# An attention, convolution and Hartley-transform kernel: its first image stacked on chip head by head, a projection on 32x32 tiles, box sums on GpSimd, fillers among the first maxima

## The chip, the cores and the metric

One core of a Trainium2 chip runs the kernel. The metric is the device time of one execution in microseconds (us), lower is better; three runs of the kernel before gave a median of 336.1 us (335.73 to 336.81).

## The reference

`x` is (4, 32, 32, 32), float32. Four blocks follow one another, each `x = x + block(norm(x))`, the norm one over each image and channel:

- block 0: a 3x3 convolution with first- and second-order (Volterra) products of its taps
- block 1: a 3x3 convolution
- block 2: one step of a convolutional LSTM whose gates come from attention
- block 3: a 2-D Hartley transform, a mix of 32x32 modes, the transform back

Block 2, which the change is about, with its hidden state at zero:

```
xin = W_in x + b_in
q = conv3x3(xin, 'SAME')        # 4 heads of 8 channels, 1024 queries
k, v = conv3x3(xin, 'VALID')    # 900 keys
a = softmax(q k) v
```

The pair (h, xin) has zero queries, so its attention is the mean of its values over all keys, a constant for each image: it needs only the nine sums of x over the 30x30 windows. Gates, cell, hidden state and `W_out` follow.

## The kernel before

There is one instruction stream for each engine; semaphores join them. An attention "half" is one image (of 4) and one half of the queries (512 of 1024), eight in all, in the order `divmod(s, 4)`: first query half of images 0 to 3, then the second.

*Front of block 2.* After the norm (`padded`, L778) TensorE projects x to `xin` (L1073 to L1079): 24 matmuls of 128 rows, one for each image, query half and vertical shift, float32, which the profile shows as two passes each. ScalarE (L644) and VectorE (L783) evict them in turn into `xst`; GpSimd blanks two edge rows (L578, L582). `conv` (L1081) then makes K, Q and V (L1098, L1101, L1108), each in two halves. The window sums of the constant are six VectorE reductions (L791, L795); three small chains of matmuls on TensorE turn them into a bias of the gates: `win_done` (L1100), 36 one-column matmuls (L1106), 12 more (L1113).

*Splitting.* So that bf16 matmuls keep float32 accuracy, Q and K are split into three bf16 parts each: ScalarE copies (L648 to L662), VectorE subtracts (L800 to L829). K is kept as its 900 keys and as the difference of its two halves. The nine products of parts are nine groups of 8 rows, 72 in all, laid out ("stacked") in `qst` and `kst`. SyncE writes the parts to DRAM (`k_scratch` L492, `q_scratch` L495) and loads the stacks from there (`stack_k` L503, `stack_q` L511), the first image in two pieces, then all others; the second query half is written (L528) and stacked last. TensorE transposes the values (L1119, L1124), and VectorE copies them out (L839 to L847), before the first maximum.

*Maxima and scores.* A softmax needs the largest score of each query. A "max block" (L1140) is 128 queries against 450 keys, four matmuls beside each other on 32-column tiles. As a pair: ScalarE takes the Relu of the difference block (L683), VectorE adds it to the first half's block and reduces (L877). The other blocks VectorE reduces alone (L882). When a half has its 16 maxima they are split, turned on TensorE (L1150), copied (`mt_sb`, L891), and one GpSimd DMA (L596) puts them below that half's queries as rows 72 to 74; its semaphore is `m_in`. Only then can the half's scores start: `score_tile` (L1169, L1174) makes 128 keys x 512 queries, ScalarE takes the exponent (L675), and `values` (L1187, L1193) accumulates in float32, 128 rows high.

*Order.* `attention_plan()` writes one list that each engine walks. It takes the 32 blocks and turn of the first half and 18 blocks of the second (`FIRST_AHEAD`), then gives each step of scores 4.15 blocks. A turn is moved behind the next four blocks (`MOVED`). `block_bank` hands out PSUM banks: six until the prologue's end, then three.

```python
    take(2 * ROWS_OF_MAX + 1 + FIRST_AHEAD)
...
                plan.append(("score", s * EXP_UNITS + t * HEADS + h))
                k = int(due * (h + 1) / units + 1e-6)
                take(k - taken)
```

`keep_clock` (L999) runs matmuls on zeros whose result nobody reads. In the last half the gates of the first query halves are worked off as items between the steps (L1244, L921 to L932).

## Time and profile before

| | us |
|---|---|
| median of three runs | 336.1 |
| the profiled execution, its own time | 335.8 |
| its span | 334.0 |
| TensorE / VectorE / ScalarE / GpSimd busy | 298.5 / 216.7 / 175.8 / 40.7 |
| mean granted clock of TensorE, 1.0 being 2.4 GHz | 0.952 |

How to read it: PE is TensorE, PEld its weight loads, DVE VectorE, ACT ScalarE, POOL GpSimd, SPq the DMA issues of SyncE. A matmul's end is modelled, so a busy TensorE is not one at its peak. In a line of the timeline stand start, duration, engine, line, operation, output and input, the count, and in brackets the idle time before it and what ended it. In a line of the windows stand the stretch and its length, then busy us and instructions of PE, PEld, DVE, ACT and POOL, the granted clock (PEclk), the mean busy share of the 16 DMA engines and GB/s. In a group's line stand the count, busy us and mean ns; a line's own view gives min/median/max ns and first and last start.

### The profile page before, as it was taken

How to read it: one execution, taken by the hardware profiler on the slowest of the kernel's cores; microseconds unless marked ns; L12 is line 12 of the kernel's file. 1: busy time of each engine (PE TensorE's matmuls, PEld its weight loads, DVE VectorE, ACT ScalarE, POOL GpSimd, SP SyncE). 2: the span in 40 equal slices, each digit the busy share in tenths (PEclk: the TensorE clock that was granted, in tenths of full speed). 3: DMA queues.
4: the chain of work that ended last, by engine and by line, in shares of the span. 5: the costliest groups of instructions: out<-in, count | busy, mean ns of one | idle time of the engine just before them, and what ended most of it. 6: DMA issues, size and time to landing. Idle time of an engine off the chain costs nothing. (4 is left out here: it accounts for less than half of the span.)

```text
span 334.0 us, 9963 instructions
## 1 busy us (share of the span) xinstructions
PE 298.5 (89%) x4276; PEld 130.9 (39%) x4283; DVE 216.7 (65%) x484; ACT 175.8 (53%) x338; POOL 40.7 (12%) x50
## 2 busy tenths in 40 slices
PE   5899979899798599999999999999997998895893
PEld 2577523234332244334334344344342223344731
DVE  3991263486497138687878878888773223779935
ACT  1201110324375479788988979889797983100000
POOL 8400000000000000100101001010200108007000
PEclk9999999999965579999999999999999999997999
DMA  7000000007796469300000000000000000000001
GB/s 265 36 4 4 7 5 1 2 0 202 169 148 109 127 182 327 140 3 4 2 5 2 3 4 2 4 4 2 4 2 4 3 0 2 0 2 2 4 0 63
DMA packets 3471, 15.40 MB, mean 46 GB/s; under 512 B 731, under 2 KB 1547, under 8 KB 2883
## 3 DMA queue, kind: packets, MB, share of 16 engines
q1 hardware_dynamic: 3171, 14.67, 16.2%
q8 instruction: 33, 0.54, 0.7%
q0 software_dynamic: 256, 0.11, 0.2%
q14 instruction: 11, 0.09, 0.1%
HBM read 12.21 MB, written 2.37 MB: 44 GB/s over the span
## 5 line engine op out<-in xcount | busy, mean ns | idle before, releaser
L675 ACT ACTIVATE arena_b<-ps 128x512 f32<-128x512 f32 x232 | 125.3, 609 | 26.2 <-PE ps L1169 24.6
L1140 PE MATMUL ps<-arena_a 72*32 72x450 bf16 x1024 | 93.7, 390 | 3.0 <-DVE vrest L847 0.8
L1169 PE MATMUL ps<-arena_a 75*32 75x512 bf16 x896 | 88.4, 390 | 6.2 <-DMA arena_a<-mt_sb 5.5
L882 DVE TENSOR_REDUCE mx<-ps 128x1 f32<-128x450 f32 x120 | 68.5, 616 | 2.8 <-PE ps L1140 2.8
L877 DVE CUSTOM_DVE_ANT_0 sums<-ps,relus 128x450 bf16<-128x450 f32 x68 | 41.8, 625 | 36.8 <-PE ps L1140 30.5
L1187 PE MATMUL ps<-arena_b,vt 128*32 128x512 f32 x448 | 59.0, 601 | 1.0 <-ACT arena_b L675 1.0
L1140 PEld LDWEIGHTS ps<-arena_a 72*32 72x32 bf16 x1024 | 28.7, 102 | 53.7 <-DVE mx L882 16.0
L1169 PEld LDWEIGHTS ps<-arena_a 75*32 75x32 bf16 x896 | 24.5, 97 | 49.8 <-ACT arena_b L675 23.1
L683 ACT ACTIVATE relus<-ps 128x450 f32<-128x450 f32 x68 | 37.5, 554 | 8.3 <-PE ps L1140 7.4
L1029 PE MATMUL ps<-arena_a,cst 32*32 32x512 f32 x864 | 28.6, 596 | 1.1 <-ACT arena_a L626 1.1
L999 PE MATMUL ps<-zeros 128*128 128x512 bf16 x82 | 21.3, 397 | 6.5 <-DMA xa<-x 3.5
L1029 PEld LDWEIGHTS ps<-arena_a,cst 32*32 32x32 f32 x864 | 20.7, 103 | 8.7 <-issue 2.6
L596 POOL DMA_DIRECT2D arena_a<-mt_sb x8 | 5.2, 651 | 104.8 <-DVE mt_sb L891 104.8
L1187 PEld LDWEIGHTS ps<-arena_b,vt 128*32 128x32 f32 x448 | 13.7, 111 | 7.4 <-ACT arena_b L675 2.3
L743 DVE SCALAR_TENSOR_TENSOR arena_a<-xp 128x612 f32<-128x612 f32 (+1 forms) x24 | 16.2, 753 | 0.0
L632 ACT ACTIVATE arena_b<-ps 128x512 f32<-128x512 f32 x4 | 2.2, 596 | 26.6 <-PE ps L1029 26.6
L1088 PE MATMUL ps<-arena_b,cst 128*32 128x450 f32 (+1 forms) x144 | 15.8, 564 | 0.0
L999 PEld LDWEIGHTS ps<-zeros 128*128 128x128 bf16 x89 | 8.0, 100 | 18.6 <-issue 7.7
L1285 PE MATMUL ps<-arena_b,arena_a 128*64 128x64 f32 x256 | 9.8, 245 | 4.7 <-DVE arena_a L458 4.6
L603 POOL TENSOR_TENSOR on<-ot,rden 128x512 f32<-128x512 f32 x7 | 7.3, 1041 | 54.4 <-DVE rden L901 54.4
L458 DVE TENSOR_TENSOR arena_a<-arena_a 32x256 f32<-32x256 f32 x24 | 12.9, 563 | 0.5
L899 DVE STREAM_TRANSPOSE ot<-ps 128x512 f32<-128x512 f32 x8 | 5.7, 713 | 10.1 <-PE ps L1193 10.1
(140 smaller groups left out, 237.3 us busy)
## 6 DMA issues: line engine op xcount, KB each, us to landing
arena_b<-wmodes SPq DMA_DIRECT2D x1, 4096.0 KB, 21.0
arena_a<-k_scratch SPq DMA_DIRECT2D x3, 516.8 KB
arena_a<-q_scratch SPq DMA_DIRECT2D x3, 384.0 KB
cst<-consts SPq DMA_DIRECT2D x1, 1045.0 KB, 8.6
k_scratch<-arena_b SPq DMA_DIRECT2D x3, 344.5 KB, 3.7
cst<-consts SPq DMA_DIRECT2D x1, 864.5 KB, 6.5
arena_a<-k_scratch SPq DMA_DIRECT2D x6, 129.2 KB
arena_a<-k_scratch SPq DMA_DIRECT2D x3, 258.4 KB
```

The lines of the kernel that those rows point to most:

```text
L458: return engine.tensor_tensor(dst, v, u, ALU.subtract if part else ALU.add)
L675: nc.scalar.activation(probs[:, n % PRING, :], ps[:, SCORE_RING[n % len(SCORE_RING)], :], ACT.Exp).then_inc(expd, 1)
L683: nc.scalar.activation(relus[:, d % 3, :], ps[:, block_bank(i), 0:KHALF], ACT.Relu).then_inc(max_relu, 1)
L743: nc.vector.scalar_tensor_tensor(maps[:, m, n0:n1], xp[:, n0:n1], VOLTERRA_SCALE, xp[:, at + n0:at + n1], ALU.mult, ALU.mult).then_inc(map ...
L877: nc.vector.tensor_tensor_reduce(out=sums[:, d % 2, :], in0=bank, in1=relus[:, d % 3, :], scale=1.0, scalar=-3.0e38, op0=ALU.add, op1=ALU.max,
L882: nc.vector.tensor_reduce(mx[:, a, e:e + 1], bank, AX.X, ALU.max).then_inc(max_read, 1)
L999: mm(ps[:, bank, :], zeros[:, 0:P], zeros[:], start=True, stop=True)
L1029: last = mm(ps[32 * j:32 * j + 32, 2 * b + e, :].rearrange("p (y x) -> p y x", x=W), l0w[r, COL_TILES * i + j, :], window(maps[r, m, :], p ...
L1088: last = mm(ps[32 * b:32 * b + 32, bank + e, 0:ny * cols].rearrange("p (y x) -> p y x", x=cols), weights[:, px, :], window(xst[:, b, :], f ...
L1140: last = mm(ps[32 * j:32 * j + 32, block_bank(i), 0:KHALF], qst[0:PAIR_ROWS, e, g, q0:q0 + 32], kst[0:PAIR_ROWS, g, at:at + KHALF], start= ...
L1169: last = mm(ps[32 * j:32 * j + 32, bank, :], kst[0:S_ROWS, g, k0:k0 + 32], qst[0:S_ROWS, e, g, :], start=True, stop=True)
L1187: last = mm(ps[32 * h:32 * h + 32, bank, :], vt[:, t, half % B * HEADS + h, :], probs[:, (n0 + h) % PRING, :], start=(t == 0), stop=False, ...
```

## The change

Constants are laid out anew: in `kst` and `k_parts` the difference stands first, then the 900 keys. The parts are:

- *Projection*: 24 matmuls on 32x32 tiles, each image's rows by its own 32x32 weights, eight banks.
- *Order of the halves*: `HALVES`, image 0's first and second query half, then images 1 to 3, first halves before second.
- *Convolutions*: Q, K, K, Q, V, V by halves, each split as soon as it is out.
- *Stacks of image 0*: straight from `q_parts` and `k_parts` on chip, one DMA for each head and part: Q heads 0 and 1 and K from SyncE, Q heads 2 and 3 from GpSimd. The last keys of K (the second 450, of use to scores only) come in twelve further DMAs. GpSimd issues the writes to DRAM. Images 1 to 3 are loaded from DRAM once the first `m_in` has landed.
- *Box sums*: 18 chained additions on GpSimd, halving the row each time, then column corrections.
- *Window chain* (mean, value, gate), bias of `W_out` (`bout`): items of the plan in the last half; gates and what follows move two steps later.
- *Values' transposes*: items among the first maxima, copied out by ScalarE, the rest by VectorE.
- *Fillers*: matmuls on zeros, 128 rows on four 32-column tiles: 256 columns behind each pair of the first half's last eight, and behind each pair of the second half's first nine; four of 512 before the first score.
- *Turn*: the first half's is no longer moved.
- *Banks*: six for the first 32 blocks, four for the 19 that follow, then three.
- `ident_b`, `mx` and the ones of `vt`, `vrest` are set on GpSimd earlier.

```diff
 KPAD = DT * P + 32
-KDIFF = KPAD
-KW = KPAD + KHALF
-K_RANGES = (slice(0, KPAD), slice(KDIFF, KW))
+KDIFF = 0
+KEY0 = KHALF
+KW = KEY0 + KPAD
+K_SECOND = slice(KEY0 + KHALF, KW)
...
 O_RING = (6, 7)
+EARLY_RING = (3, 4, 5, 7, 0, 2)
+AHEAD_RING = (3, 4, 5, 7)
+XIN_BANKS = (0, 1, 2, 6, 3, 4, 5, 7)
+K_BANKS, Q_BANKS, V_BANKS = (0, 1), (2, 6), (0, 1)
+VT_TILES = 3
...
 FIRST_AHEAD = 18
-WIDE_AHEAD = 12
 BLOCKS_PER_STEP = 4.15
 MOVED = 4
+AMONG_FIRST = {2: (("vt", 0),), 3: (("vt_copy", 0),), 6: (("vt", 1),), 7: (("vt_copy", 1),)}
+PAIRED = 2
+FILLS_BEFORE = 4
 MODE_STAGES = [(k2, lh) for k2 in range(2) for lh in range(2)]
...
             for kind in (("diff", "first") if pair else ("first", "second")):
                 stream.append(("max", i, s, a, kind))
                 i += 1
+            if s == 0:
+                stream += AMONG_FIRST.get(a, ())
+            if s == 0 and a > max(AMONG_FIRST):
+                stream.append(("fill", 256))
         stream.append(("split", s))
         stream.append(("turn", i, s))
...
-    take(2 * ROWS_OF_MAX + 1 + FIRST_AHEAD)
+    take(2 * ROWS_OF_MAX + 1)
+    for _ in range(FIRST_AHEAD // 2):
+        take(2)
+        plan.append(("fill", 256))
+    plan += [("fill", 512)] * FILLS_BEFORE
     due, prev, later, step = 0.0, None, [], 0
...
-                    later += [(step + 1, ("gates", 0)), (step + 2, ("cell", 0)), (step + 3, ("hidden", 0)),
-                              (step + 4, ("out", 0))]
+                    later += [(step, ("window", "mean")), (step, ("bout",)), (step + 1, ("window", "value")),
+                              (step + 2, ("window", "gate")), (step + 3, ("gates", 0)), (step + 4, ("cell", 0)),
+                              (step + 5, ("hidden", 0)), (step + 6, ("out", 0))]
...
-            ring = SCORE_RING + MAX_RING if i < prologue else MAX_RING
+            last = 2 * ROWS_OF_MAX
+            ring = EARLY_RING if i < last else AHEAD_RING if i < last + 1 + FIRST_AHEAD else MAX_RING
...
+            def stack_q_head(g):
+                for s in range(PARTS):
+                    sp.dma_start(qst[part_rows(s), 0, g, :],
+                                 q_parts[HC * g:HC * (g + 1), s, 0:HALF].unsqueeze(1).to_broadcast([HC, PARTS, HALF])
+                                 ).then_inc(q_head[g], 16)
...
+            def stack_k_head(g, cols, signal):
+                for s in range(PARTS):
+                    sp.dma_start(kst[part_rows(s), g, cols], k_parts[HC * g:HC * (g + 1), :, cols]).then_inc(signal, 16)
...
+            for s in range(PARTS):
+                sp.wait_ge(q_part[s], 1)
+            for g in range(2):
+                stack_q_head(g)
             for s in range(PARTS):
                 sp.wait_ge(k_part[s], 2)
-                if s == 0:
-                    sp.wait_ge(k_zeroed, 2)
-                sp.dma_start(k_dram[:, s].rearrange("c g n -> g c n"), k_parts[:, s, :]).then_inc(kd_written, 16)
+            for g in range(HEADS):
+                stack_k_head(g, slice(0, K_SECOND.start), k_head[g])
+            sp.wait_ge(qd_written[1], PARTS * 16)
+            stack_q(1, 0, HEADS, q_second)
+            sp.wait_ge(k_padded, 1)
+            sp.wait_ge(k_zeroed, 1)
             for s in range(PARTS):
-                sp.wait_ge(q_part[s], 1)
-                sp.dma_start(q_dram[s, 0].rearrange("c g n -> g c n"), q_parts[:, s, 0:HALF]
-                             ).then_inc(qd_written[0], 16)
...
+                sp.wait_ge(k_part[s], 3)
+            for g in range(HEADS):
+                stack_k_head(g, K_SECOND, k_second)
+            sp.wait_ge(m_in, 16)
             sp.wait_ge(kd_written, PARTS * 16)
-            stack_k(0, 0, HEADS // 2)
             sp.wait_ge(qd_written[0], PARTS * 16)
-            stack_q(0, 0, 0, HEADS)
-            stack_k(1, HEADS // 2, HEADS)
...
-            stack_q(3, 1, 0, G)
+            for b in range(1, B):
+                stack_k(b)
+                stack_q(0, HEADS * b, HEADS * (b + 1), q_in[b - 1])
+            stack_q(1, HEADS, G, q_in_second)
             sp.wait_ge(ones_in, 16)
-            sp.wait_ge(m_in, 16)
+            for g in range(HEADS):
+                sp.wait_ge(q_head[g], PARTS * 16)
+                sp.wait_ge(k_head[g], PARTS * 16)
+            sp.wait_ge(k_second, HEADS * PARTS * 16)
             sp.dma_start(wm, wmodes).then_inc(wm_loaded, 16)
...
+            pool.wait_ge(vt_zeroed, 2)
+            nc.gpsimd.memset(vt[:, :, :, HC:HC + 1], 1.0).then_inc(vt_zeroed, 1)
+            for h in range(HEADS):
+                pool.wait_ge(vt_zeroed, 3 + h)
+                nc.gpsimd.memset(vrest[32 * h:32 * h + KREST, :, 32 * h + HC:32 * h + HC + 1], 1.0
+                                 ).then_inc(vt_zeroed, 1)
...
+            nc.gpsimd.memset(k_parts[:, :, KEY0 + KEYS:KW], 0.0).then_inc(k_zeroed, 1)
+            nc.gpsimd.memset(mx[:], -3.0e38).then_inc(mx_ready, 1)
+            pool.wait_ge(consts_loaded, 16)
+            nc.gpsimd.tensor_copy(ident_b[:], c_("ident")).then_inc(mx_ready, 1)
...
-            pool.wait_ge(vt_ready, 2 + HEADS)
             pool.wait_ge(xin_ready, 2)
-            nc.gpsimd.memset(vt[:, :, :, HC:HC + 1], 1.0).then_inc(vt_zeroed, 1)
...
+            def win_link(out, a, b, op):
+                win_steps[0] += 1
+                nc.gpsimd.tensor_tensor(out, a, b, op).then_inc(win_step, 1)
+                pool.wait_ge(win_step, win_steps[0])
...
+            win_link(cols[:, :, 0:n], image[:, :, 0:n], image[:, :, n:2 * n], ALU.add)
+            while n > 1:
+                n //= 2
+                win_link(cols[:, :, 0:n], cols[:, :, 0:n], cols[:, :, n:2 * n], ALU.add)
+            for v, (x0, x1) in enumerate(((30, 31), (0, 31), (0, 1))):
+                win_link(wsum[:, v, :].unsqueeze(2), image[:, :, x0:x0 + 1], image[:, :, x1:x1 + 1], ALU.add)
+            win_link(wsum[:], cols[:, :, 0:1].rearrange("p y x -> p x y").to_broadcast([P, 3, H]), wsum[:], ALU.subtract)
...
+            for s in range(PARTS):
+                pool.wait_ge(q_part[s], 1)
+            for g in range(2, HEADS):
+                for s in range(PARTS):
+                    pool.dma_start(qst[s * PARTS * HC:(s + 1) * PARTS * HC, 0, g, :],
+                                   q_parts[HC * g:HC * (g + 1), s, 0:HALF].unsqueeze(1).to_broadcast([HC, PARTS, HALF])
+                                   ).then_inc(q_head[g], 16)
+            for s in range(PARTS):
+                pool.dma_start(q_dram[s, 0].rearrange("c g n -> g c n"), q_parts[:, s, 0:HALF]).then_inc(qd_written[0], 16)
+            for s in range(PARTS):
+                pool.wait_ge(q_part[s], 2)
+                pool.dma_start(q_dram[s, 1].rearrange("c g n -> g c n"), q_parts[:, s, HALF:HW]).then_inc(qd_written[1], 16)
+            for s in range(PARTS):
+                pool.wait_ge(k_part[s], 3)
+                pool.dma_start(k_dram[:, s].rearrange("c g n -> g c n"), k_parts[:, s, :]).then_inc(kd_written, 16)
...
+            first, diff, second = (slice(KEY0, KEY0 + KHALF), slice(KDIFF, KDIFF + KHALF), slice(KEY0 + KHALF, KEY0 + KEYS))
+            act.wait_ge(q_done, 1)
+            q_copy(0, 0, ps[:, Q_BANKS[0], :])
+            act.wait_ge(q_left, 1)
+            q_copy(1, 0, q_res[:, 0:HALF])
+            act.wait_ge(k_done, 1)
+            nc.scalar.activation(k_first, ps[:, K_BANKS[0], 0:KHALF], ACT.Copy).then_inc(k_copied, 1)
+            act.wait_ge(k_copied, 1)
+            k_copy(0, first, k_first)
+            act.wait_ge(k_left, 1)
+            k_copy(1, first, k_res[:, first])
+            act.wait_ge(k_left, 2)
+            k_copy(0, diff, k_res[:, diff])
             act.wait_ge(k_done, 2)
...
-                act.wait_ge(dve_step, Q_RESID[e])
-                nc.scalar.activation(q_parts[:, 1, half], q_res[:, half], ACT.Copy).then_inc(q_part[1], 1)
-            act.wait_ge(v_done, 2)
...
-            nc.scalar.activation(vs.rearrange("p (a n) -> p a n", a=2), ps[:, 6:8, 0:KHALF],
-                                 ACT.Copy).then_inc(vs_ready, 1)
+            k_copy(0, second, ps[:, K_BANKS[1], 0:KHALF])
+            act.wait_ge(k_left, 3)
+            k_copy(1, diff, k_res[:, diff])
+            act.wait_ge(q_done, 2)
+            q_copy(0, 1, ps[:, Q_BANKS[1], :])
+            act.wait_ge(k_left, 4)
+            k_copy(1, second, k_res[:, second])
+            act.wait_ge(q_left, 2)
+            q_copy(1, 1, q_res[:, HALF:HW])
+            v_copy(0)
+            v_copy(1)
             for item in plan:
                 if item[0] == "score":
...
+            dve.wait_ge(q_part[0], 1)
+            q_rest_of(0)
+            dve.wait_ge(q_part[1], 1)
+            q_last(0)
+            dve.wait_ge(k_part[0], 1)
+            k_rest_of(first, k_first, 0)
+            dve.wait_ge(k_done, 2)
+            nc.vector.tensor_tensor(k_res[:, diff], ps[:, K_BANKS[1], 0:KHALF], k_first, ALU.subtract).then_inc(k_left, 1)
+            dve.wait_ge(k_part[1], 1)
+            k_last(first)
+            dve.wait_ge(k_part[0], 2)
+            dve.wait_ge(k_left, 2)
+            k_rest_of(diff, k_res[:, diff], 0)
+            dve.wait_ge(k_part[1], 2)
+            dve.wait_ge(k_left, 3)
+            k_last(diff)
+            dve.wait_ge(k_part[0], 3)
+            k_rest_of(second, ps[:, K_BANKS[1], 0:KHALF], 0)
+            dve.wait_ge(q_part[0], 2)
+            q_rest_of(1)
+            dve.wait_ge(k_part[1], 3)
+            dve.wait_ge(k_left, 4)
+            k_last(second)
+            dve.wait_ge(q_part[1], 2)
+            dve.wait_ge(q_left, 2)
+            q_last(1)
             def split_max(s):
...
+            def keep_clock_tiled(bank, n):
+                for j in range(COL_TILES):
+                    mm(ps[32 * j:32 * j + 32, bank, 0:n], zeros[:, 0:32], zeros[:, 0:n], start=True, stop=True)
...
-                e, b = divmod(n, B)
+            for e in range(2):
                 for r in range(3):
-                    last = mm(ps[32 * r:32 * r + 32, (2 + n) % 8, :].rearrange("p (y x) -> p y x", x=W),
-                              c_("win")[:, 32 * b:32 * b + 32],
-                              window(xp, r, 1, 16 * e, 16, W), start=True, stop=True)
-                last.then_inc(xin_done, 1)
-            def conv(bank, weights, rows, cols, first, signal):
+                    for b in range(B):
+                        rows = slice(32 * b, 32 * b + 32)
+                        last = mm(ps[32 * r:32 * r + 32, XIN_BANKS[e * B + b], :].rearrange("p (y x) -> p y x", x=W),
+                                  c_("win")[rows, rows], window(xp[rows], r, 1, 16 * e, 16, W), start=True, stop=True)
+                        if r == 2:
+                            last.then_inc(xin_done, 1)
...
+            pe.wait_ge(xin_ready, 1)
+            conv(Q_BANKS[0], qkv[:, 0], H, W, 0, q_done, 0)
+            conv(K_BANKS[0], qkv[:, 1], KH, KH, 1, k_done, 0)
+            pe.wait_ge(xin_ready, 2)
+            conv(K_BANKS[1], qkv[:, 1], KH, KH, 1, k_done, 1)
+            conv(Q_BANKS[1], qkv[:, 0], H, W, 0, q_done, 1)
+            pe.wait_ge(k_copied, 1)
+            conv(V_BANKS[0], qkv[:, 2], KH, KH, 1, v_done, 0)
+            pe.wait_ge(k_left, 4)
+            conv(V_BANKS[1], qkv[:, 2], KH, KH, 1, v_done, 1)
...
+            def of_window(what):
+                bank = WIN_BANKS[("mean", "value", "gate").index(what)]
+                if what == "mean":
+                    pe.wait_ge(win_step, WIN_STEPS)
+                    for i in range(len(MAX_RING)):
+                        pe.wait_ge(*blocks_read[turn_of[2 * B - 1] - i])
+                    mm(ps[:, bank, 16:25], c_("win"), win9[:, 0, :], start=True, stop=True).then_inc(win_done, 1)
...
+            def turn_values(part):
+                if part == 0:
+                    pe.wait_ge(vs_ready, 1)
+                    pe.wait_ge(q_left, 2)
+                    for t in range(VT_TILES):
+                        last = nc.tensor.transpose(ps[:, 6, t * P:(t + 1) * P], vs[:, t * P:(t + 1) * P], c_("ident"))
+                else:
...
                     max_block(*item[1:])
                 elif item[0] == "turn":
                     turn_maxima(*item[1:])
+                elif item[0] == "vt":
+                    turn_values(item[1])
+                elif item[0] == "fill":
+                    if not fills:
+                        pe.wait_ge(vt_ready, 2)
+                    fills.append(item)
+                    keep_clock_tiled(V_BANKS[1], item[1])
...
+                            if bank in EARLY_RING:
+                                pe.wait_ge(*blocks_read[block_before(2 * ROWS_OF_MAX, bank)])
+                        pe.wait_ge(vt_ready, 2)
+                        pe.wait_ge(vrest_ready, HEADS)
                         pe.wait_ge(vt_zeroed, 3 + HEADS)
+                        pe.wait_ge(k_second, HEADS * PARTS * 16)
```

## Rows read from the trace of the kernel before

**Rows 1.** Windows by stage, columns as told in the profile section.
```profile
59.98:88.97 28.99, 26.66 (x307) 10.76 (x309) 16.73 (x33) 9.29 (x14) 1.00 (x3) 1.00 0.35 94
88.97:112.59 23.62, 17.45 (x202) 5.91 (x202) 15.97 (x56) 13.45 (x25) 1.39 (x6) 0.60 0.73 129
112.59:134.20 21.61, 21.45 (x274) 9.15 (x278) 11.07 (x32) 18.14 (x37) 0.60 (x1) 0.80 0.76 238
134.20:255.80 121.60, 118.18 (x1814) 46.96 (x1804) 97.06 (x234) 105.65 (x208) 10.07 (x12) 1.00 0.03 10
255.80:276.30 20.50, 19.24 (x214) 5.63 (x206) 4.46 (x7) 17.86 (x35) 1.05 (x2) 1.00 0.01 2
```

**Rows 2.** Timeline, all engines, from the first split to the first values.
```profile
100.17 0.19 DVE L854 TENSOR_REDUCE negm<-mx 128x16 f32<-128x32 f32 x1
...
102.79 0.79 POOL L596 DMA_DIRECT2D arena_a<-mt_sb  x1 [12.99 <-DVE mt_sb L891]
...
112.62 0.62 PE L1169 MATMUL ps<-arena_a 75*32 75x512 bf16 x4 [5.17 <-DMA arena_a<-mt_sb]
...
118.19 1.95 PE L1187 MATMUL ps<-arena_b,vt 128*32 128x512 f32 x8
```

**Rows 3.** The DMAs that carry the turned maxima, line 596.
```profile
L596 POOL DMA_DIRECT2D arena_a<-mt_sb x8: 603/637/785, 102.8 to 254.8; - x8
...
DMA to landing us min/median/max: 2.0/2.8/9.6
```

**Rows 4.** Timeline from the projection to the first maxima.
```profile
59.98 6.66 PE L1076 MATMUL ps<-xp,cst 128*32 128x512 f32 x45 [1.31 <-DVE xp L728]
...
62.06 0.75 DVE L783 TENSOR_SCALAR arena_b<-ps,cst 96x512 f32<-96x512 f32 x1 [2.13 <-PE ps L1076]
...
72.83 5.36 PE L1088 MATMUL ps<-arena_b,cst 128*32 128x512 f32 x48
...
80.18 4.84 PE L1088 MATMUL ps<-arena_b,cst 128*32 128x450 f32 x48
...
88.97 1.51 PE L1140 MATMUL ps<-arena_a 72*32 72x450 bf16 x28 [0.77 <-DVE vrest L847]
```

**Rows 5.** The page's groups: the first convolution.
```profile
L1029 PE MATMUL ps<-arena_a,cst 32*32 32x512 f32 x864 | 28.6, 596 | 1.1 <-ACT arena_a L626 1.1
```

**Rows 6.** Timeline of the splitting of the query projection.
```profile
78.47 0.63 ACT L662 ACTIVATE arena_b<-arena_b 128x512 bf16<-128x512 f32 x1 [1.45 <-DVE arena_b L822]
...
79.20 0.69 DVE L829 TENSOR_TENSOR arena_b<-arena_b 128x512 bf16<-128x512 f32 x1 [0.77 <-ACT arena_b L662]
```

**Rows 7.** SyncE's issues of the key stacks, line 503.
```profile
L503 SPq DMA_DIRECT2D arena_a<-k_scratch x12: 342/365/462, 81.6 to 90.5; - x12
```

**Rows 8.** Timeline of the window matmuls.
```profile
78.12 2.13 PE L1106 MATMUL ps<-win,cst 32*32 32x1 f32 x72
```

**Rows 9.** Timeline, VectorE's reads of maxima, at either clock.
```profile
91.22 0.62 DVE L877 CUSTOM_DVE_ANT_0 sums<-ps,relus 128x450 bf16<-128x450 f32 x1
91.76 0.62 DVE L877 CUSTOM_DVE_ANT_0 sums<-ps,relus 128x450 bf16<-128x450 f32 x1
...
96.50 0.63 DVE L877 CUSTOM_DVE_ANT_0 sums<-ps,relus 128x450 bf16<-128x450 f32 x1
...
97.25 0.63 DVE L877 CUSTOM_DVE_ANT_0 sums<-ps,relus 128x450 bf16<-128x450 f32 x1
```

**Rows 10.** Windows, TensorE alone: busy, clock, DMA share, GB/s.
```profile
94.00:98.00 4.00, 4.00 (x48) 0.50 1.06 168
...
121.00:124.00 3.00, 3.00 (x52) 0.98 1.09 284
```

**Rows 11.** GpSimd's normalisation by form, and VectorE's mode parts beside GpSimd's.
```profile
L603 POOL TENSOR_TENSOR on<-ot,rden 128x512 f32<-128x512 f32 x7 | 7.3, 1041 | 54.4 <-DVE rden L901 54.4
...
L458 DVE TENSOR_TENSOR arena_a<-arena_a x24: 409/417/940, 300.7 to 313.7; 32x256 f32<-32x256 f32 x24
```

**Rows 12.** The page's DMA issues: key stack of one image.
```profile
arena_a<-k_scratch SPq DMA_DIRECT2D x3, 258.4 KB
```

348 lines of the change are left out of this document (171 added, 177 removed).

## The prediction

> **What bounds the kernel now.** I read the windows by stage first [rows 1]. From 134.2 to 255.8 us TensorE is busy 118.2 of 121.6 us at full clock: six halves of the attention loop, 20.3 us each, run at what the engine can do. The weak stage is 88.97 to 112.59, the first maxima alone: TensorE 17.5 of 23.6 us, mean clock 0.60, DMA share 0.73. Then I read the timeline where it ends [rows 2]. GpSimd issues the DMA with the first turned maxima at 102.79, and the first score waits for it until 112.62. Its landing is the slowest of eight, 9.6 us against a median of 2.8 [rows 3]; it shares the DMA engines with the stacks of all images. Before this stage the first maximum starts at 88.97 [rows 4], behind the projection (from 59.98), three convolutions, the splitting, the trip through DRAM and the transposes of the values. The loop has no slack, so the end moves with the start of the first score, T1 = 112.6.
>
> **Projection to first maximum.** 24 matmuls of 128 rows take 6.66 us [rows 4]. On 32x32 tiles the nearest row is the first convolution, 864 passes in 28.6 us, 33 ns each [rows 5]. Twelve matmuls are 24 passes, 0.8 us, and about 0.3 us until the first arrives: one half is out at 61.1, both by 62. Now the evictions bound it: VectorE's four at 0.75 [rows 4] end at 61.1 + 3.1 = 64.2 with their handovers, ScalarE's four beside them. Two on each engine and GpSimd's small memset, some 0.3 (three instructions take 1.00 us there [rows 1]), release the first convolution at 63.1 instead of 66.1.
> TensorE then runs Q, K, K, Q, V, V. A half of 512 columns costs 2.6 (5.36 for two [rows 4]), one of 450 costs 2.4 (4.84 for two [rows 4]). Ends: 65.7, 68.1, 70.5, 73.1, 75.5, 77.9.
> The splits are links of 0.63 on ScalarE and 0.69 on VectorE [rows 6], each behind the other. First Q half: four links from 65.7, ready at 68.4. K's first half and the difference: the last needs K's second half (70.5), then five links, the engines crossing, so 73.8. The V convolutions wait for the copy of K's first half and for its last remainder (74.4); both are there before TensorE is. SyncE then issues twelve K copies. A K stack's issue takes 0.37 [rows 7], GpSimd's up to 0.79 [rows 3]; I take 0.5, nearer the first. Head 0's three are out at 75.3 and land by the median of 2.8 at 78.1; bounds 77.9 (TensorE) and 85 (at 9.6). With the engines nearly empty I take the median. Maxima start at **78.1**, 10.9 us earlier. Window matmuls (2.13 us [rows 8]) and value transposes no longer stand in front.
>
> **First half's maxima.** Sixteen pairs at 0.55, VectorE's start to start at full clock [rows 9], 8.7 us; the first read comes 1 us after the first matmul; two value copies on ScalarE (0.63 each as in [rows 6]) add 1.2, with VectorE's rest copies beside them. End 89.0. A pair costs TensorE 0.75 at half clock, where it is never idle (4.0 of 4.0 us [rows 10]), so 0.38 at full; it idles 0.17 of 0.55, and a filler of 256 columns (0.11) fits: nothing. Split, turn and copy took from 100.17 to 102.79 with two reads between [rows 2]; without them 1.6: 90.6. As the turn is no longer moved behind later blocks, TensorE stands still for some 1.3 us of that.
>
> **Queues.** GpSimd's 18 box-sum steps read 1300 elements a partition: at 2.0 ns (512 in 1.04 us [rows 11]) and 0.2 a step 6.2 us, so 64.9 to 71.1. Lower bound 2.7 (by elements alone), upper 18.7 (1.04 for every step). Most steps have under 100 elements, so I take 6.2; the upper end would make head 2 land at 88 where it is wanted at 83, 5 us lost. Behind the sums stand six Q head copies, six Q writes and three K writes, 15 issues at 0.64 [rows 3], out by 81. The second Q half's write has landed by 84, SyncE stacks it by 89, wanted at 90.6: a cover of 1.6 us; if it goes, each us late is a us of T1. K's last columns, twelve more copies, land by 95. Behind SyncE's new wait for the first m_in stand all stacks of images 1 to 3. M_in: 90.6 + 0.64 + 2.2 = 93.5 on a quiet queue (2.0 to 9.6 [rows 3]).
>
> **Second half's maxima.** Nine pairs before the first score. With four banks a pair needs its predecessors' back, which I estimate at 0.62 a pair: 5.6 us, and four fillers of 512 columns 0.85. **T1 = 97.0**, 15.6 us earlier; bounds 93.5 (m_in) and 103 (m_in at 9.6).
>
> **After T1.** (a) Until 121 the clock was at half [rows 10]. Still the first half took only 21.6 us against 20.3 later [rows 1], because ScalarE is nearly as full: at full clock it gives back 1.3 (bounds 0 and ScalarE's idle 3.5). (b) The window chain moves into the last half, where ScalarE is busy 17.9 of 20.5 us and fed by TensorE [rows 1]: 2.13 + 0.6 us of one-column matmuls, of which the score banks hide about 1: 1.7 lost (bounds 0 and 2.8). VectorE has 16 idle us there: bias add and small copies cost nothing. (c) Image 1's stacks, 3 x (258.4 [rows 12] + 96) KB, at 129 GB/s [rows 1] take 8.2 us from 95: there by 106, wanted at 108. The second m_in is issued near 110 among the others; at 9.6 us it lands at 120, wanted at 118: 1.0 lost (bounds 0 and 2).
>
> **Sum.** 335.8 (the profiled execution; its span is 334.0) - 15.6 - 1.3 + 1.7 + 1.0 = 321.6. The runs' median is 336.1, so plus 0.3: **321.9 us**.
>
> [...] From 94 to 98 TensorE is never idle at half clock and stays there; before it fell it had run maxima for 0.38 of each 0.55 us, behind pauses. Four-pass matmuls come in at 118.19 [rows 2], and by 121 the clock is up [rows 10]. Whether the fillers hold it among maxima no row shows, hence two rivals, and by these rows a clock once lost stays lost to the first values. [...]
>
> **Rivals.**
> 1. *The clock falls in the turn's gap,* 89 to 91. For: it fell at 94 after the pauses between 85.0 and 88.97 [rows 4] and thin maxima. Against: fillers on both sides. At half clock a pair with its filler is 0.75 + 0.21 = 0.96: nine pairs cost 3.1 more, the four fillers 0.85, and (a) is lost, 5.2 together: **327.1**.
> 2. *It falls among the first eight pairs,* which have no fillers; two rounds of four-pass transposes speak against. Ten more pairs at 0.96 add 4.0: **331.1**.
> 3. *Slower: GpSimd's queue.* M_in stands behind 15 issues of d us: T1 = 71.1 + 15d + 2.9. With (a) lost, break-even is at T1 = 109.9, d = 2.4. Against: eight issues took 0.60 to 0.79 beside VectorE's maxima [rows 3]. For: those moved 12 KB each, and a VectorE operation with two inputs in SBUF went from 0.41 to 0.94 us beside GpSimd [rows 11], so the two do block each other. At d = 3 T1 is 118.9 and the time **345**. The Trainium skill (SBUF — State Buffer, A bandwidth-pool intuition that's wrong) has such a DMA go from about 620 to 3100 ns beside a VectorE copy; by that figure the time would be about 346, an estimate. No row here shows it.
> 4. *Better:* the pairs pack tighter and m_in alone sets T1 = 93.5, 3.5 less: **318.4**.
> 5. *The stacks come late:* head or second-half stacks share the DMA engines with the K writes and each is 2 us later: **326**, inside the range.
>
> **How the numbers follow.** Forecast 0.42, rival 1 0.22, rival 2 0.12, rival 3 0.04, rival 4 0.08, rival 5 0.12. Rivals 1 and 5 lie above, so the range is lopsided: 316.5 (rival 4 with its 2 us of spread) to 331.5 leaves out rival 3, half of rival 2 and the tails. A measurement of this kernel tells about 0.3%, 1 us, from no change. Faster 0.94, same 0.02, slower 0.04: only GpSimd's queue near or beyond d = 2.4 is not faster.
>
> **What would show it.** First maximum near 78; VectorE's reads 0.55 apart to 89; the second m_in landing late. Granted clock 1.0 from 78 to 130, or 0.5 from about 91 (rival 1) or 83 (rival 2). GpSimd's issues near 0.64 and m_in issued right behind the copy, or rival 3. First score near 97, and from there to the last score about 165 us (163.2 now, 112.6 to 275.8). The forecast is wrong if that length changes by over 3 us, or if the heads land after 80.

## The result, and the profile after

The kernel with the change takes **336.28 us** (median of 20 runs, 333.14 to 341.14), the kernel before, measured beside it, 337.37 (20 runs, 335.73 to 341.93). The ratio is **0.9934**, 95% interval 0.9906 to 0.9963: 0.7% faster, where 4.2% was forecast. The time lies above the range. Ratios, here and below, are taken over undisturbed runs and medians over all, so the two need not agree exactly.

| us | before | forecast | after (profiled) |
|---|---|---|---|
| profiled execution / span | 335.8 / 334.0 | | 337.8 / 336.0 |
| projection starts | 59.98 | 59.98 | 61.60 |
| first maximum | 88.97 | 78.1 | 80.20 |
| GpSimd issues the first maxima DMA | 102.79 | 90.6 | 100.57 |
| first score, T1 | 112.6 | 97.0 | 109.8 |
| first to last score, the loop | 163.2 | about 165 | 168.5 |

T1 is 12.8 later than forecast and the loop 3.5 longer: 321.6 + 12.8 + 3.5 = 337.9, the profiled execution. By the table the 12.8 are 2.1 at the first maximum, 7.9 from there to the DMA's issue (forecast 12.5, now 20.4) and 2.8 from that to T1 (6.4, now 9.2).

Windows by stage, the kernel after; columns as in [rows 1]:

```profile
59.93:80.20 20.27, 17.16 (x194) 5.26 (x193) 10.90 (x18) 9.76 (x17) 13.21 (x29) 1.00 0.15 24
80.20:90.00 9.80, 5.07 (x83) 2.66 (x87) 5.35 (x20) 4.80 (x10) 3.93 (x8) 0.94 0.78 217
90.00:100.50 10.50, 8.53 (x106) 4.53 (x105) 6.18 (x22) 4.40 (x9) 0.00 (x0) 0.50 0.26 62
100.50:109.79 9.29, 9.29 (x120) 4.65 (x116) 5.71 (x18) 4.90 (x9) 0.62 (x1) 0.52 0.57 118
...
131.00:152.00 21.00, 17.08 (x230) 6.42 (x234) 12.85 (x32) 13.43 (x27) 1.48 (x2) 0.84 0.46 153
```

The first line is the part that came out about as forecast. In the second, where the sixteen pairs should be going at 0.55 each, TensorE is busy for only half of the time while the DMA engines are busy for 0.78 of it. From 89, inside that hole in TensorE's work, the clock is at its lower level, 1.2 GHz, until the first score. The last line holds a second hole. TensorE's timeline shows both:

```profile
61.60 2.21 PE L1212 MATMUL ps<-xp,cst 32*32 32x512 f32 x48 [1.34 <-DVE xp L850]
64.76 14.62 PE L1222 MATMUL ps<-arena_b,cst 128*32 128x512 f32 x144 [0.95 <-POOL arena_b L629]
80.20 0.57 PE L1296 MATMUL ps<-arena_a 72*32 72x450 bf16 x8 [0.82 <-DMA arena_a<-arena_b]
...
89.87 0.94 PE L1296 MATMUL ps<-arena_a 72*32 72x450 bf16 x8 [4.24 <-issue]
...
99.74 0.28 PE L1306 MATMUL ps<-ident_b,mparts 128*32 128x128 bf16 x2 [1.97 <-DVE mparts L967]
...
109.79 0.40 PE L1323 MATMUL ps<-arena_a 75*32 75x512 bf16 x4
...
134.84 0.62 PE L1323 MATMUL ps<-arena_a 75*32 75x512 bf16 x4 [3.88 <-DMA arena_a<-mt_sb]
```

The projection is down from 6.66 us [rows 4] to 2.21. Before the first pair of head 2, at 89.87, TensorE stands still for 4.24 us with no releaser named; the turn's gap is 1.97; and at 134.84 a score waits 3.88 for the second half's maxima DMA (of which the group of line 687 says the same: it landed 11.1 us after its issue, where before the slowest was the first, 9.6 [rows 3]).

```profile
L687 POOL DMA_DIRECT2D arena_a<-mt_sb x8: 616/624/646, 100.6 to 254.9; - x8
...
DMA to landing us min/median/max: 2.0/2.1/11.1
```

GpSimd's queue, where the slower rival was looked for, in its timeline:

```profile
66.07 1.32 POOL L641 TENSOR_TENSOR on<-xp 128x512 f32<-128x512 f32 x1
67.47 1.97 POOL L641 TENSOR_TENSOR on<-on 128x256 f32<-128x256 f32 x4
...
75.80 3.62 POOL L670 DMA_DIRECT2D arena_a<-arena_b  x6 [0.31 <-POOL win L641]
79.38 1.62 POOL L674 DMA_DIRECT2D q_scratch<-arena_b  x3
80.99 1.57 POOL L677 DMA_DIRECT2D q_scratch<-arena_b  x3
82.56 1.57 POOL L680 DMA_DIRECT2D k_scratch<-arena_b  x3
```

Fifteen issues in 8.3 us, 0.56 each: the queue is fast. But see what it issues when: from 79.38 to 84.13 nine writes to DRAM. Now SyncE in the same stretch (line 531: key columns of one head and one part, on chip):

```profile
70.42 4.33 SPq L524 DMA_DIRECT2D arena_a<-arena_b  x6
75.50 13.34 SPq L531 DMA_DIRECT2D arena_a<-arena_b  x12
88.88 2.64 SPq L544 DMA_DIRECT2D arena_a<-q_scratch  x3
91.71 8.55 SPq L531 DMA_DIRECT2D arena_a<-arena_b  x12
```

Twelve copies, three for each head in turn, take 13.34 us: the first seven 0.7 each, the other five, from 80.50 on, 1.0 to 2.7. By this head 2's third copy was issued by 83.2, and its first pair still stood until 89.87, with nothing in the wait list that says why. That its keys landed late is an inference here. Whether SyncE's issue by itself is slow or the writes slow the copies is what the first experiment asks.

### The profile page after: what moved, and what is told of

Same layout as the page of the kernel before. It is cut to its first block and busy times, and to the rows that moved or that the text cites. A ratio compares the mean times of both kernels' runs of the same rounds, so it can differ in the third digit from the quotient of the medians.

```text
span 336.0 us, 10195 instructions
## 1 busy us (share of the span) xinstructions
PE 296.6 (88%) x4358; PEld 134.4 (40%) x4364; DVE 212.4 (63%) x476; ACT 176.7 (53%) x343; POOL 57.7 (17%) x84
## 3 DMA queue, kind: packets, MB, share of 16 engines
HBM read 11.12 MB, written 2.37 MB: 40 GB/s over the span
## 5 line engine op out<-in xcount | busy, mean ns | idle before, releaser
L1296 PE MATMUL ps<-arena_a 72*32 72x450 bf16 x1024 | 95.3, 389 | 6.9 <-issue 4.7
L1323 PE MATMUL ps<-arena_a 75*32 75x512 bf16 x896 | 86.8, 386 | 4.7 <-DMA arena_a<-mt_sb 3.9
L1343 PE MATMUL ps<-arena_b,vt 128*32 128x512 f32 x448 | 58.1, 593 | 0.5 <-ACT arena_b L786 0.5
L1296 PEld LDWEIGHTS ps<-arena_a 72*32 72x32 bf16 x1024 | 29.4, 102 | 54.3 <-issue 20.8
L1323 PEld LDWEIGHTS ps<-arena_a 75*32 75x32 bf16 x896 | 23.8, 96 | 45.0 <-ACT arena_b L786 20.1
L1164 PE MATMUL ps<-arena_a,cst 32*32 32x512 f32 x864 | 30.1, 627 | 1.7 <-ACT arena_a L717 1.7
L1164 PEld LDWEIGHTS ps<-arena_a,cst 32*32 32x32 f32 x864 | 22.2, 105 | 9.2 <-issue 4.3
L1222 PE MATMUL ps<-arena_b,cst 128*32 128x450 f32 (+1 forms) x144 | 14.6, 562 | 0.9 <-POOL arena_b L629 0.9
L1457 PEld LDWEIGHTS ps<-arena_b,arena_a 128*64 128x64 f32 x256 | 9.3, 159 | 5.7 <-issue 4.4
```

The lines of the kernel that those rows point to most:

```text
L1164: last = mm(ps[32 * j:32 * j + 32, 2 * b + e, :].rearrange("p (y x) -> p y x", x=W), l0w[r, COL_TILES * i + j, :], window(maps[r, m, :], p ...
L1296: last = mm(ps[32 * j:32 * j + 32, block_bank(i), 0:KHALF], qst[0:PAIR_ROWS, e, g, q0:q0 + 32], kst[0:PAIR_ROWS, g, at:at + KHALF], start= ...
L1323: last = mm(ps[32 * j:32 * j + 32, bank, :], kst[0:S_ROWS, g, k0:k0 + 32], qst[0:S_ROWS, e, g, :], start=True, stop=True)
L1343: last = mm(ps[32 * h:32 * h + 32, bank, :], vt[:, t, HALVES[half][1] * HEADS + h, :], probs[:, (n0 + h) % PRING, :], start=(t == 0), stop ...
L1457: last = mm(banks(4 * k2, 4)[64 * jh:64 * jh + 64, 64 * l:64 * l + 64], xv[:, k2, l, jh], wv[:, k2, l, jh], start=True, stop=True)
```

## The experiments

Theory A: the writes to DRAM share the DMA engines with the copies that heads 2 and 3 wait for; the hole of 4.24 us then drops the clock, and the second hole is the bulk stacks and the mode weights in front of the second maxima DMA. Rivals: SyncE's issue of small copies is slow by itself; the clock would be low anyway.

**1. Writes behind the copies** (six of the nine writes, those of the first query half and of the keys, wait in GpSimd's queue until every head's first keys have landed; the second query half's three, which SyncE stacks next, stay in front).

```diff
-            (the three writes of q_dram[s, 0])
             (the three writes of q_dram[s, 1])
+            for g in range(HEADS):
+                pool.wait_ge(k_head[g], PARTS * 16)
+            (the three writes of q_dram[s, 0])
             for s in range(PARTS):
                 pool.wait_ge(k_part[s], 3)
```

> Theory A (the first-half Q and the K writes to DRAM, issued by GpSimd from 79 to 84, share the DMA engines with the K head copies and make head 2 late by 4.2 us): with these six writes behind the landing of all heads the stall at head 2 (4.24 us before the read at 89.87) goes below 1 us, first maximum stays near 80, first score comes 4 us or more earlier, and if the clock then holds through the maxima about 10 us earlier. Rival B (SyncE's own issue of twelve copies at 0.7 to 2.7 us each sets it): the stall stays at 3 us or more, first score within 1 us of 109.8. Rival C: the writes now late delay the stacks of image 1 and the gain is given back at the third half.

Measured: 329.77 us (328.27 to 333.3), ratio 0.975 (0.970 to 0.980). TensorE's timeline at head 2, and GpSimd's first held write, which waits for the last of the heads:

```profile
83.39 0.57 PE L1298 MATMUL ps<-arena_a 72*32 72x450 bf16 x8
84.36 0.56 PE L1298 MATMUL ps<-arena_a 72*32 72x450 bf16 x8 [0.40 <-issue]
...
87.17 1.57 POOL L679 DMA_DIRECT2D q_scratch<-arena_b  x3 [7.68 <-DMA arena_a<-arena_b]
```

The hole is gone, and the same copies are in time from the same queue; SyncE now issues them in 10.30 us instead of 13.34. The six writes were the cause, and SyncE's slow issue was in part their effect. Which of the two groups of three does the harm was not parted. T1 is 101.6, 8.2 earlier, though 1.5 of this is another matter: in some executions, the profiled one of after among them, the clock is at half at 10 to 13 us, and the projection starts at 61.6 instead of 60.1. How much of the medians' 6.5 us that is, is open. The clock still falls, at 93, behind the turn's gap.

**2. Bulk transfers behind the maxima DMAs.** **3. Both.**

```diff
             for b in range(1, B):
+                sp.wait_ge(m_in, b * 16)
                 stack_k(b)
                 stack_q(0, HEADS * b, HEADS * (b + 1), q_in[b - 1])
+            sp.wait_ge(m_in, 4 * 16)
             stack_q(1, HEADS, G, q_in_second)
...
+            sp.wait_ge(m_in, 5 * 16)
             sp.dma_start(wm, wmodes).then_inc(wm_loaded, 16)
```

> Theory: the second m_in landed 11.1 us after its issue because the stacks of images 2 and 3 and the 4 MB of mode weights shared the engines; issued behind the second to fifth m_in they leave it alone. Then it lands in 2 to 3 us, the 3.9 us stall and the half clock behind it (134 to 140) go, and the kernel is 4.5 to 6 us faster than the changed one (ratio to before near 0.98). Rival: the stacks of image 1 or the slow path of GpSimd's DMA keep it above 8 us; time unchanged.

> If the two delays are independent the gains add: 4 + 5 us against the changed kernel without the clock, about 15 us if the clock holds from 80 to 100 (326 to 322 us). If the clock falls all the same at the turn or the head wait, 327 to 329.

Measured: 2 alone 333.58 us (331.51 to 334.25), ratio 0.987 (0.982 to 0.992); both **327.39** (326.61 to 327.75), ratio 0.969 (0.966 to 0.973). In both the slowest maxima DMA lands in under 4 us, the lines of run 2:

```profile
L690 POOL DMA_DIRECT2D arena_a<-mt_sb x8: 616/624/646, 100.9 to 248.6; - x8
...
DMA to landing us min/median/max: 2.0/2.1/3.9
```

The second hole was the DMA engines too: in run 2's profiled execution the loop is 161.9 us instead of 168.5, with the clock up throughout. By the medians run 2 gained only 2.7 us on the kernel after, where 4.5 to 6 were expected; its profiled execution is the fastest of its four. With both, T1 is 101.94 and the loop 165.3, the forecast's 165, though not from its terms, as told below. What is left is the clock. Run 3's windows and timeline about the turn:

```profile
90.00:92.00 2.00, 0.02 (x2) 0.05 (x2) 1.66 (x9) 0.02 (x1) 0.03 (x1) 1.00 0.96 268
92.00:94.00 2.00, 1.93 (x34) 0.92 (x38) 1.02 (x4) 1.18 (x3) 0.62 (x1) 0.74 0.77 263
94.00:98.00 4.00, 4.00 (x52) 1.86 (x52) 2.59 (x9) 2.06 (x5) 0.00 (x0) 0.50 0.26 56
```
```profile
91.98 0.23 PE L1311 MATMUL ps<-ident_b,mparts 128*32 128x128 bf16 x2 [2.37 <-DVE mparts L972]
...
95.41 0.97 PE L1301 MATMUL ps<-arena_a 72*32 72x450 bf16 x8
96.17 0.43 PE L1132 MATMUL ps<-zeros 128*32 128x256 bf16 x4
96.38 0.97 PE L1301 MATMUL ps<-arena_a 72*32 72x450 bf16 x8
```

This is rival 1 of the prediction as written: 2.37 us without work, then the clock at half, and pairs 0.97 apart (0.96 was forecast for that case, and 327.1 us).

**4. Both, and no fillers.**

> As e3 without any filler matmul. If the fillers hold the clock, the clock is 0.5 here from about 90 on and the first score comes 3 to 6 us later than in e3. If they do not hold it, every pair at half clock costs 0.75 us instead of 0.96 and the first score comes 0.21 x 17 + 1.7 = 5.3 us earlier than in e3. If the clock holds in both, equal within 1 us.

Measured: 326.9 us (325.37 to 328.44), ratio 0.966 (0.962 to 0.971). The time is that of run 3, but not for want of an effect. The clock fell earlier, at 88.8, and came back later, at 116. Without fillers the nine pairs at half clock take 7.27 us, 0.81 each. The first of these lines is of the windows:

```profile
88.00:90.00 2.00, 1.74 (x24) 0.71 (x28) 2.00 (x9) 1.29 (x3) 1.35 (x3) 0.69 0.46 137
...
93.94 7.27 PE L1297 MATMUL ps<-arena_a 72*32 72x450 bf16 x72
102.32 0.62 PE L1324 MATMUL ps<-arena_a 75*32 75x512 bf16 x4 [1.11 <-DVE mx L984]
```

This fall is in the middle of the first half's pairs, 5 us ahead of the turn at 93.82 (this front ran 1.6 late); run 3's came at 93.0, behind its turn's gap. By these two executions the fillers held the clock among the first half's pairs, and the turn's gap then lost it all the same. What they give there they take among the nine pairs, 0.97 each instead of 0.81. The first score came 1.2 us sooner after the projection than in run 3, not the 5.3 expected.

**5. The turn's gap filled** (added to run 3).

```diff
         stream.append(("split", s))
+        if s == 0:
+            stream += [("fill", 512)] * 10
```

> Both moves of the run before (DRAM writes behind the head stacks, bulk stacks behind the maxima transfers), and ten 512-column fillers between the last maxima pair of the first half and its turn, where TensorE stood idle for 2.37 us. Clock theory: it is that gap that drops the granted clock at 93 to 103; filled, the clock stays at 1.0, the nine pairs of the second half take about 0.62 instead of 0.97 each, the first score comes near 98.5 instead of 101.9, and the time is about 324 (ratio to before 0.96). Rival: the stretch of maxima itself lets the clock fall, filled gap or not, since the run without fillers and the run with them gave the same time: first score at 101.5 to 102, time 327. A second rival: fillers run into the turn's slot and cost what they save.

Measured: **322.28 us** (320.87 to 324.66), ratio **0.959** (0.952 to 0.965). TensorE's timeline, then the windows:

```profile
89.25 2.44 PE L1134 MATMUL ps<-zeros 128*32 128x256 bf16 x44
91.92 0.23 PE L1313 MATMUL ps<-ident_b,mparts 128*32 128x128 bf16 x2 [0.22 <-DVE mparts L974]
...
98.21 1.15 PE L1134 MATMUL ps<-zeros 128*32 128x256 bf16 x20
100.20 0.40 PE L1330 MATMUL ps<-arena_a 75*32 75x512 bf16 x4 [0.85 <-DMA arena_a<-arena_b]
```
```profile
94.00:98.00 4.00, 3.41 (x72) 1.24 (x64) 3.32 (x13) 3.00 (x7) 0.00 (x0) 1.00 0.32 74
```

The same work as run 3, but for 40 matmuls on zeros in a time in which TensorE had nothing to do, and the clock stays at 1.0 from before the turn to 247 us. The turn starts as early as without them (91.92 against 91.98), so they cost nothing. The first score waits now for a DMA, the last key columns, which SyncE issues in 11.66 us. T1 missed the expected 98.5 by 1.7; 0.9 of it is this wait, by run 9. Whether the fillers among the pairs are still of use once the turn is filled, no run tried.

**6. The projection back on 128 rows** (on run 3). **7. The order of halves of before** (on run 3). **8. The kernel before, with its bulk transfers held back.**

```diff
-                        rows = slice(32 * b, 32 * b + 32)
                         last = mm(...
-                                  c_("win")[rows, rows], window(xp[rows], r, 1, 16 * e, 16, W), ...
+                                  c_("win")[:, 32 * b:32 * b + 32], window(xp, r, 1, 16 * e, 16, W), ...
```
```diff
-HALVES = ((0, 0), (1, 0), (0, 1), (0, 2), (0, 3), (1, 1), (1, 2), (1, 3))
+HALVES = ((0, 0), (0, 1), (0, 2), (0, 3), (1, 0), (1, 1), (1, 2), (1, 3))
... (image 1's stacks no longer wait for an m_in, images 2 and 3 for one less)
```
```diff
+            sp.wait_ge(m_in, 16)
             stack_k(3, 2 * HEADS, G)
             stack_q(2, 0, 2 * HEADS, G)
+            sp.wait_ge(m_in, 2 * 16)
             (writes and stacks of the second query half)
-            sp.wait_ge(m_in, 16)
+            sp.wait_ge(m_in, 3 * 16)
             sp.dma_start(wm, wmodes).then_inc(wm_loaded, 16)
```

> Both moves kept, and the input projection back on 128-row weights (24 matmuls that contract all 128 rows, each with one image's columns) instead of 32x32 tiles. Theory: the projection is paced by its matmuls one after another, so the stretch from padded input to first maximum grows from about 18.7 to some 21.5 us (24 x 0.21 instead of 2.2 us), and everything after it moves with it: first score near 104.7, time 330 (ratio 0.977). Rival: the evictions of the eight banks pace that stretch, and only 1 us or less is lost: 328.

> Both moves kept, but the halves again in the order of before: the first halves of all four images, then the second ones; image 1's stacks are issued right after the second key columns and wait for no maxima. Theory: what the new order buys is that the pairs ahead of the first score need nothing but the on-chip copies of image 0; with the old order they wait for a DRAM round trip that SyncE issues at about 97, land near 102, and the first score comes at 110 to 113, time 336 to 338 (ratio about 1.0). Rival: the order matters little, since the clock is low there anyway: first score by 104, time below 330.

> The kernel of before, with its bulk transfers put behind its maxima transfers: stacks of images 2 and 3 behind the first, second query half behind the second, mode weights behind the third. Theory: before's first maxima transfer landed 9.6 us after its issue because those stacks were on the DMA engines; held back, it lands in 3 to 6 us, the first score comes at 106 to 109 instead of 112.6, and the time is 331 to 334 (ratio 0.98 to 0.99). Rival: the transfer is late from image 1's stacks alone, which stay where they are, and nothing changes: 337.

Measured, 6: 336.47 us (333.08 to 342.09), ratio 0.995 (0.990 to 0.999), all of the gain of run 3 gone. The projection in its timeline:

```profile
60.11 11.08 PE L1216 MATMUL ps<-xp,cst 128*32 128x512 f32 x45 [1.34 <-DVE xp L855]
```

11.08 us, not the expected 5 and not the 6.66 of before (the time expected was 330). The loops stand in the new order, in which all four images of one shift write the same 32 output partitions one after another; run 11 tests whether it is that.

Measured, 7: 341.84 us (339.69 to 342.99), ratio 1.015 (1.009 to 1.022). The maxima of image 1 wait for its stacks through DRAM, 15.46 us long, and T1 is 118.1, where 110 to 113 was expected (and 336 to 338 us):

```profile
107.78 0.94 PE L1301 MATMUL ps<-arena_a 72*32 72x450 bf16 x8 [15.46 <-DMA arena_a<-q_scratch]
```

So the new order of the halves is what lets the on-chip stacking pay: with image 0's copies alone, 16 us of T1 hang on it. This is this kernel's front with image 1 written late, not the front of before.

Measured, 8: 333.26 us (332.68 to 337.58), ratio 0.988 (0.983 to 0.992). T1 is 106.1, as expected, so the first maxima DMA was late because of the bulk stacks. But first to last score grew from 163.2 to 171.5: the stacks held back are now themselves late, and the clock is at half for 13 us behind that wait:

```profile
120.65 0.57 PE L1142 MATMUL ps<-arena_a 72*32 72x450 bf16 x4 [3.03 <-DMA arena_a<-q_scratch]
```

The profiled execution is the slowest of the eight (337.6 us); the 4 us that the median gained have no trace of their own. Either way, part of what the change yields was to be had without it.

**9. The last key columns on two queues; 10. the window chain early; 11. the wide projection in the order of before** (each on run 5).

```diff
-            for g in range(HEADS):
+            for g in range(HEADS // 2):
                 stack_k_head(g, K_SECOND, k_second)
... (GpSimd issues heads 2 and 3; its K and first-half Q writes go behind its first m_in)
```
```diff
+        if 4 <= n < 8:
+            plan.append(("value_of", n - 4))
+        else:
+            plan.append(("fill", 256))
... (the mean behind pair 3, the gate's behind pair 9, in the place of FILLS_BEFORE)
```
```diff
-                for r in range(3):
-                    for b in range(B):
+                for b in range(B):
+                    for r in range(3):
```

> Built on the run with the turn's gap filled (322.28 us, first score at 100.20, after 0.85 us of idle TensorE and 2 us behind the last pair, waiting for the last key columns, whose twelve copies SyncE issues in 11.66 us). Here GpSimd issues six of the twelve, in the time that it spent on K writes and first-half Q writes, which go behind its first maxima transfer. Theory: SyncE's issue of those copies is what sets the first score now; on two queues they are there before TensorE is done, the first score comes at 98.7 to 99, and the time is about 321 (ratio 0.954). Rival: the copies are slow because of the DMA engines, not of the queue, and split copies land no earlier: no gain, 322 or above.

> Built on the run with the turn's gap filled. The window chain leaves the last half: the mean goes behind the third pair of the second half's maxima, its one-column value matmuls, a quarter at a time, behind pairs five to eight in the place of fillers, the gate's before the first score, in the place of four fillers of 512 columns. Theory: in the last half its 3.1 us of one-column matmuls cost 1.7 us and the clock after them (0.5 for 3 to 6 us, about 1 us more); ahead of the first score there are 2 us in which TensorE only waits for the last key columns. First score at 100 to 101, first to last score 3 us shorter (162.2 now), time about 320 (ratio 0.951). Rival: one-column matmuls among the pairs let the clock fall there, the pairs take 0.96, first score at 103 or later, and the time is 323 or more.

> Built on the run with the turn's gap filled, with the input projection on 128-row weights as before and also in the order of before (image outside, row shift inside). The last undoing of this part kept the new order, in which twelve neighbouring matmuls write the same 32 partitions, and its projection took 11.08 us. Theory: matmuls of different 32-partition outputs overlap and those of the same one do not; in the old order the projection takes the 6.66 us that it took in the kernel before, the first maximum comes 4.4 us later than with 32x32 tiles, at 83, and the time is about 326.5 (ratio 0.971). Rival: the projection is as long as in that run, whatever the order, and the time 331.

Measured, 9: 323.75 us (321.04 to 326.53), ratio 0.949 (0.937 to 0.961). The columns are there in time and T1 is 99.33, without a wait:

```profile
98.36 1.15 PE L1145 MATMUL ps<-zeros 128*32 128x256 bf16 x20
99.33 0.39 PE L1341 MATMUL ps<-arena_a 75*32 75x512 bf16 x4
```

The wait is gone, and T1 with it 0.9 us earlier. That it was SyncE's queue is not shown: the run also took the six writes out of this stretch, and SyncE's six copies took 0.71 us each, where run 5's twelve took 0.97. Nor does the gain stand out of the spread: two of the four runs took 326.4 and 326.5 us, the other two 321.0 and 321.1, and the fastest is not faster than run 5's.

Measured, 10: 327.59 us (325.49 to 328.25), ratio 0.967 (0.958 to 0.976), where 320 was expected. The rival holds. TensorE's timeline:

```profile
97.26 0.72 PE L1271 MATMUL ps<-win,cst 32*32 32x1 f32 x18
97.91 0.57 PE L1312 MATMUL ps<-arena_a 72*32 72x450 bf16 x8
98.41 0.72 PE L1271 MATMUL ps<-win,cst 32*32 32x1 f32 x18
99.06 0.84 PE L1312 MATMUL ps<-arena_a 72*32 72x450 bf16 x8
99.84 1.12 PE L1271 MATMUL ps<-win,cst 32*32 32x1 f32 x18
```

From 96 on the engine is busy throughout, but with one-column matmuls between the pairs, and the clock falls at 99: a group goes from 0.72 to 1.12 us. T1 is 104.7 in a profile whose front was 1.5 late.

Measured, 11: 328.58 us (325.37 to 330.14), ratio 0.968 (0.957 to 0.979). The projection:

```profile
61.59 6.66 PE L1218 MATMUL ps<-xp,cst 128*32 128x512 f32 x45 [1.34 <-DVE xp L857]
```

To the hundredth what it was before. Same matmuls, other order, 6.66 against 11.08. In this order neighbours write different 32 partitions of one bank; in run 6's, four in a row write the same 32 partitions in four banks. (The expectation says twelve in a row; it is four, each in two passes.) Partition and bank changed together, and no run parts them. From the start of the projection to the first maximum it is 22.3 us, against 18.6 in the kernel after: the narrow tiles are worth 3.7. The median is 2 us above the expected 326.5; the profiled execution had the clock at half in its front, which put everything 1.5 us later.

**12. The pause in the front filled** (on run 9).

```diff
                     mm(ps[:, 4 + b, :], zeros[r, 0:P], zeros[r, :], start=True, stop=True)
+            keep_clock(7, 6)
```

> Built on the run with the last key columns on two queues, whose times fell into two groups, 321.1 and 326.5 us. Where a profile of this family has the granted clock at 0.5 at 10 to 14 us, right behind a pause of 1.6 to 1.7 us in TensorE's work, everything after it is 1.5 us later; so six more 512-column fillers go into that pause. Theory: this fall is one of those that part the groups; the first maximum then always starts at 78.8, the first score at 99 to 99.4, and the median is 321 to 322 (ratio 0.948 to 0.955) with a spread under 4 us. Rival: the falls come wherever they come (the clock also falls in the last half or not), the front is not the place, and the median stays at 323 to 324 with the same two groups.

Measured: 325.79 us (323.14 to 331.95), ratio 0.963 (0.958 to 0.968). The theory fails, and the time is above the rival's 323 to 324 too. The profiled execution has no fall at the front, but falls at 247 and 291 us, and the runs are further apart than before. Whether the fillers do harm somewhere is open.

## Why the prediction was wrong, point by point

Right:

- *Projection to first maximum.* From the projection's start 18.6 us, forecast 18.1. The narrow tiles cost 2.21 (about 2 forecast), and undoing them in the old order loses 3.7 where 3.0 was forecast.
- *GpSimd's issues:* 0.56, forecast 0.64; rival 3 is out: the longest of the fifteen took 0.80 us, the longest maxima issue 646 ns. The case that spoke for it in the Trainium skill (SBUF — State Buffer, A bandwidth-pool intuition that's wrong: 620 ns become 3100 beside a VectorE copy) did not arise. VectorE was at work beside these issues, but with subtractions and reductions, most of them out of PSUM, and with no copy, so they do not test the page's figure.
- *Pairs* at 0.55 at full clock and 0.96 at half: 0.55 in run 5 once no hole is in them, 0.97 in run 3. The second half's nine, estimated at 0.62, came at 0.66 in run 5.

Wrong, with what it cost:

- **"Queues", the step that failed first.** "Behind the sums stand six Q head copies, six Q writes and three K writes, 15 issues at 0.64 [rows 3], out by 81." I costed the issues and asked what stands behind them on their own queue, not what they do to transfers of another queue on the same DMA engines. Head 2 was late by the hole of 4.24 us, which is gone once six of the writes are held back (run 1). Rival 5 named this mechanism, but for the K writes alone, at 2 us, without the clock that went with it and inside the range. The box sums came out at 9.4 us, not 6.2; with the writes moved (run 1) nothing is seen to wait for that. The last key columns, forecast to land by 95, held the first score until 100.2 in run 5: their issues took 0.97 us each, not 0.5.
- **"Second half's maxima", the clock.** I took it that the fillers hold the clock, with a gap of "some 1.3 us" in which TensorE stands still. The gap is 1.97 to 2.37, and the clock does not survive it: rival 1. Its price of 5.2 is near the 5.1 between the medians of runs 3 and 5, but not by its terms: it put 3.9 of it ahead of T1, which moved by 1.7 (2.6 with run 9). It got 0.22; the row that should have raised it was my own, that the clock of before fell behind pauses. In the kernel after, the clock fell first, at 88.9, inside the hole of head 2. Of the 7.9 us above, 4.2 are that hole and the other 3.7 mostly the pairs of heads 2 and 3 at half clock; the 2.8 behind the turn are the nine pairs at 0.96.
- **(c), mis-sized.** The text on record: "at 9.6 us it lands at 120, wanted at 118: 1.0 lost". It landed after 11.1, TensorE stood still for 3.88, and the clock was at half from 133.3 to 140.1. By the 161.9 of an undisturbed loop in runs 2 and 9, the two cost 168.5 - 161.9 = 6.6 us. A stall has to be priced with the clock that it takes along.
- **(a) and (b) together.** Forecast -1.3 + 1.7 = +0.4; run 9's loop, with the clock up throughout, is 161.9, so -1.3. The two were not parted: run 10, with the chain out of the loop but 8.2 us of half clock in it, has 162.3. And a term is missing: the clock can fall behind the chain's one-column matmuls in the last half. Half clock for 0, 3.4, 6.8 and 8.1 us in the loops of runs 9, 5, 11 and 3 went with 161.9, 163.5, 165.1 and 165.3, about 0.45 us for each us. It costs less at the loop's start: run 4 has 13.8 us of it there and a loop of 166.6. Why it falls in one execution and not in another stays open.

The gain that the prediction counted was there. Of 14 us between 336.3 and run 5's 322.3, the writes account for 6.5 (some of it perhaps the front's clock), the bulk transfers for 2.4 on top, the turn's gap for 5.1. That 322.3 is so near the forecast 321.9 is partly luck: T1 is 3.2 later than I had it, the loop 1.5 shorter, and the median of the runs 0.9 below the profiled execution.

## What to carry to other kernels

When copies are taken off a DRAM round trip, look at what else the change issues at that moment on any queue: writes that nothing waits for yet will run ahead of copies that everything waits for. Put them behind a semaphore of the urgent ones; here that is four waits for 6.5 us, some of it perhaps the front's clock. Put a filler first where TensorE stands still longest ahead of a stretch that it bounds: ten in the turn's gap were worth 5.1 us and cost nothing. Those among the pairs held the clock up to that gap and bought nothing while the gap was open. And price a stall twice: its own length, and the half-clock stretch behind it.
